# Moving fill-in work to earlier steps of an attention loop, and alternating its PSUM bank

## The reference

```python
def reference(x, w_qkv, w_out, w_up, w_down):      # x: (8, 4096, 1024), float32
    x = layernorm(x + attention(x, w_qkv, w_out))  # 16 heads of 64, causal softmax
    h = gelu(ternary_linear(x, w_up))              # rms-normalised input, weights -1/0/1
    x = layernorm(x + ternary_linear(h, w_down))   # d_ff = 4096
    return x
```

## Time and profile before

| | us |
|---|---|
| median of 3 runs | 3507.16 |
| lowest, highest | 3487.97, 3547.02 |
| profiled execution | 3440.04 |
| its span, slowest core | 3438.5 |

### The profile page before, as it was taken

One profiled execution on the slowest core, in us unless ns is written; L12 is line 12 of the kernel. 1 busy time (PEld: TensorE's weight loads), 2 busy tenths in 40 slices (PEclk: granted clock), 3 DMA queues, 4 the chain that ended last, 5 costly groups with the idle time before them and its releaser, 6 DMA issues. The chain is left out here.

```text
span 3438.5 us, 52708 instructions; the slowest of 8 cores (3428.3 to 3438.5 us)
## 1 busy us (share of the span) xinstructions
PE 2666.4 (78%) x19808; PEld 1328.1 (39%) x19808; DVE 970.6 (28%) x2483; ACT 1857.3 (54%) x2165; POOL 116.0 (3%) x231
## 2 busy tenths in 40 slices
PE   5995456677777777777777788334599999999998
PEld 2443123233333344344334444222344444444444
DVE  5443343333332322321211110454411111111111
ACT  2453113346576777777887888355443434443443
POOL 0000000000000000000000000000000000000000
PEclk9998667677777877878887755656699999999999
DMA  6666101010100101001000000343311111111111
GB/s 135 156 159 140 31 7 50 13 50 13 38 26 20 44 1 38 26 1 38 26 1 13 26 13 1 116 156 106 90 41 37 47 47 44 34 47 47 46 31 37
DMA packets 54922, 171.26 MB, mean 50 GB/s; under 512 B 6545, under 2 KB 6546, under 8 KB 54674
## 3 DMA queue, kind: packets, MB, share of 16 engines
q1 hardware_dynamic: 37730, 134.33, 12.2%
q0 software_dynamic: 16944, 33.56, 6.3%
HBM read 167.87 MB, written 33.55 MB: 59 GB/s over the span
## 5 line engine op out<-in xcount | busy, mean ns | idle before, releaser
L38 ACT ACTIVATE p_sb<-sc,negC 128x1024 bf16<-128x1024 f32 (+3 forms) x1152 | 1162.2, 1041 | 506.1 <-PE pvB L38 489.4
L38 PE MATMUL sc<-QT,KT 64*128 64x512 bf16 (+3 forms) x2304 | 530.8, 453 | 193.2 <-ACT p_sb L38 189.3
L38 PE MATMUL dwn<-wdnT,hTs 128*128 128x512 bf16 x2048 | 459.1, 380 | 8.8 <-ACT hTs L38 8.8
L38 PE MATMUL upq<-wupT,x1Ts 128*128 128x512 bf16 x2048 | 454.0, 380 | 6.5 <-DVE x1Ts L38 2.0
L38 PE MATMUL pvA<-VS,p_sb 128*128 128x65 bf16 x4224 | 372.9, 215 | 57.0 <-DVE recs L38 24.6
L38 PE MATMUL pvB<-VS,p_sb 128*128 128x65 bf16 x4224 | 375.5, 216 | 39.1 <-DVE attO L38 39.1
L38 PEld LDWEIGHTS pvA<-VS,p_sb 128*128 128x128 bf16 x4224 | 220.5, 107 | 396.6 <-issue 393.2
L38 ACT ACTIVATE h_sb<-upq,r_all 128x512 bf16<-128x512 f32 x256 | 175.2, 685 | 227.5 <-PE upq L38 224.6
L38 PEld LDWEIGHTS upq<-wupT,x1Ts 128*128 128x128 bf16 x2048 | 198.5, 98 | 256.5 <-issue 23.3
L38 PEld LDWEIGHTS dwn<-wdnT,hTs 128*128 128x128 bf16 x2048 | 195.8, 98 | 233.8 <-issue 15.7
L38 PEld LDWEIGHTS sc<-QT,KT 64*128 64x128 bf16 x2304 | 132.8, 96 | 374.6 <-issue 346.0
(11 more groups left out here) (107 smaller groups left out, 1874.2 us busy)
## 6 DMA issues: line engine op xcount, KB each, us to landing
wr<-w_up SPq DMA_DIRECT2D x64, 512.0 KB, 4.8
wr<-w_down SPq DMA_DIRECT2D x64, 512.0 KB, 4.1
xb<-x POOLq DMA_DIRECT2D x64, 256.0 KB, 3.9
xfy<-x SPq DMA_DIRECT2D x32, 512.0 KB, 3.4
x1spill<-xfy SPq DMA_DIRECT2D x32, 512.0 KB, 2.6
x1f<-x1spill SPq DMA_DIRECT2D x32, 512.0 KB, 5.4
out<-outs SPq DMA_DIRECT2D x32, 512.0 KB, 6.2
x1b<-x1spill POOLq DMA_DIRECT2D x32, 256.0 KB, 3.6
```

The lines of the kernel that those rows point to most:

```text
L38: getattr(self.real, op)(*args, **kw))
```

## The change

The bank of the transposes alternates: tiles with even number in the chunk go to bank 0, odd ones to bank 1, in `emit_qtrans`, `emit_proj_trans` and the preamble of chunk 0. Items are drained from k = 2 on instead of k = 5, and where nj > 16 at even steps instead of odd ones; budgets are as before. And before an `emit_proj_mm` of tile ti, `force_ln` emits the waiting layernorm items up to tile ti - 2, so that the load of xfy for which it waits has been issued.

```diff
@@ emit_qtrans, and alike in emit_proj_trans and the preamble of chunk 0
+                    mk = "mm6" if tt % 2 == 0 else "mm7"
+                    mo = 1024 * (tt % 2)
-                    t.wait(st2["mm6"])
+                    t.wait(st2[mk])
-                        t.transpose(mmp_b[:, 128 * ch:128 * ch + 128],
+                        t.transpose(mmp_b[:, mo + 128 * ch:
+                                          mo + 128 * ch + 128],
-                                  mmp_b[:, 0:1024].rearrange(
+                                  mmp_b[:, mo:mo + 1024].rearrange(
-                    st2["mm6"] = ("qxTe", ti)
+                    st2[mk] = ("qxTe", ti)
@@
+                def force_ln(ti):
+                    def tkey(q):
+                        return 4 * q[0][1] + q[0][2] if q else 10 ** 9
+                    while min(tkey(pend_ln), tkey(pend_ln2)) <= ti - 2:
+                        q = pend_ln2 if tkey(pend_ln2) <= tkey(pend_ln) \
+                            else pend_ln
+                        f2, c2, t2 = q.pop(0)
+                        f2(c2, t2)
@@ drain_in, and alike in drain_end
+                        if fn is emit_proj_mm:
+                            force_ln(4 * cc + tt)
@@
-                            elif p >= 1 and k >= 5 and (k % 2 == 1
+                            elif p >= 1 and k >= 2 and (k % 2 == 0
                                                         or nj <= 16):
                                 drain_end(p - 1,
                                           budget=(2 if nj <= 12 else 1))
```

More of the change, by code:

```diff
@@ L522, in emit_proj_trans @@
                     v.tensor_copy(aTs[:, ti % 2],
-                                  mmp_b[:, 0:1024].rearrange(
+                                  mmp_b[:, mo:mo + 1024].rearrange(
                                       "p (c n) -> p c n", n=128))
                     v.mark(("aTe", ti))
-                    st2["mm6"] = ("aTe", ti)
+                    st2[mk] = ("aTe", ti)
                 def emit_proj_mm_a(cc, tt):
@@ L636, in phase2 @@
                                    x_hbm[128 * ti:128 * ti + 128, :])
+                            mk = "mm6" if tt % 2 == 0 else "mm7"
+                            mo = 1024 * (tt % 2)
                             t.wait(("xb2", ti))
                             t.wait(("c", 6))
-                            t.wait(st2["mm6"])
+                            t.wait(st2[mk])
                             for ch in range(8):
                                 t.transpose(
-                                    mmp_b[:, 128 * ch:128 * ch + 128],
+                                    mmp_b[:, mo + 128 * ch:
+                                          mo + 128 * ch + 128],
                                     xb2[:, ti % 2, 128 * ch:128 * ch + 128],
```

## The result

The changed kernel takes **0.9855 of the time before, with a 95% interval from 0.9832 to 0.9877**: 1.45% faster, some 50 us. The medians are 3470.8 us against 3487.79; they also hold executions in which one half of the chip ran at a lower clock, which the ratio leaves out (those of the changed kernel that it keeps took 3388.68 to 3396.28 us). The profiled execution took 3392.37 us, against 3440.04. The forecast was -38.5 us, 1.1%, from the same sum. What it called the limit of a measurement, 2%, was too coarse: the interval above is 0.45% wide.

A forecast was written before the change was run, and what follows sets the result against it. ScalarE's exps set the pace, with 506 us idle before them. The terms summed to -38.5 us: 3401.5 from the profiled 3440.04, or 3468 on the median's scale, 1.95% higher; range 3405 to 3530 us.

The forecast's parts named there:

- the limit of a measurement, 2%: Whole kernel: a measurement can tell about 2% from no change, 70 us.
- Chunk 0: Items moved from the chunk's end into pairs 1 to 7: 35.4 us saved, pairs lengthened, -11.7 us net.
- Chunks 1 and 2: Earlier items cost less in the pairs and chunk 1's bare end shrinks: -11.2 and -7.1 us.
- The chain through y: Pair 2: next chunk's first transposes wait for the projection's scale, spill and reload, holding up scores; +18 us.
- Rival (c): Pair 2: the wait for y costs double, also holding masks and the next copy; 3487 us, chance 0.14.
- the clock: Pair starts: TensorE's higher clock may return one item earlier; -7 us, an eighth of 56.
- the next M now takes the 1.0 to 1.7: Chunks 3 to 6: step 2's matmul item is nearly hidden, the next costs 1.0 to 1.7; regular pairs win 0.3 us.
- a bound of 56: Most the clock could bring if it never fell at pair starts: 2 us in each of about 28 pairs.
- without a gap from T - 1 to about T + 7.5: Pair start: TensorE works unbroken at 1.2 GHz over this stretch; T is the end of the previous pair's last products.
- Rival (a): Pair starts: the clock stays up because the moved matmuls fill TensorE's idle 2 us; -88 us, 3418 us, chance 0.17.
- Rival (b): Regular pairs of chunks 1 to 6: the clock no longer comes back; 3526 us, up to 3555, chance 0.14.
- The bank: Preamble, chunk 1's pair 0 and the end: alternating banks spare second transposes' 0.94 us wait for the copy; -2.9 us.

The follow-up runs named there:

- e1: Kernel before with only the alternating bank and `force_ln` added, items drained at the old steps; 0.9975 of the kernel before.
- e7: Changed kernel, next chunk's four `emit_qtrans` items ahead of the last projection tile from chunk 1's pairs on; no ratio, fastest execution 3361.77 us against 3388.68.
- E5: Changed kernel with items of nj > 16 drained at even steps from 4 instead of from 2; 0.9952 of the kernel before.
- e6: Changed kernel with items of nj > 16 drained at odd steps from 3; 1.0011 of the kernel before.
- e10: Kernel before plus four unread matmuls at step 2 in pairs 4 to 7 of chunks 4 to 6, no item moved; 0.9969 of the kernel before.
- e4: Changed kernel plus four unread matmuls at each of steps 2 and 4 in pairs 3 to 7 of chunk 7; 0.9806 of the kernel before.
- e2: Changed kernel with early draining only where nj > 16 (chunks 4 to 7), short chunks from step 5; 0.9933 of the kernel before.

## Why the prediction came out as it did

**Chunk 0: right in kind, too large.** -11.7 forecast for the moved items, -9.5 measured; e1 gives 3.0 of it to the bank, so the items alone won 6.5. Pairs take 9.9 us (10.4 forecast), some 16 us without exps remain at the end (12 to 15). The pair with the Xs was mis-sized: 14.7 instead of 10.3 us. I had counted the third and fourth load, 4 us from their buffers, but not that the first two are issued by POOL behind its masks of pair 0, at 412.17, and land at 416.9.

**Chunks 1 and 2: the sum right by luck**, -17.1 measured for -16.3 with the chain. The bare 8.4 us between chunks 1 and 2 are gone (1.6), and C costs 2.3 inside (2.8 forecast; 8.4 less 2.8 is 5.6, not the 5.2 of the sum). Pairs 4 to 7 of chunk 1 fell from 19.5, 16.3, 19.4, 24.3 to 13.3, 11.9, 11.3, 14.5: more than the 3.1-for-5.2 of the forecast, since V N cost 1.0 there and the M M of pairs 6 and 7 run at 1.00. These four pairs won 28.5 us, where the block's -8.4 and C's -5.2 had been counted. That paid for pairs 2 and 3, 35.5 and 26.8 us instead of 26.3 and 18.4, 17.7 more, where some +4 had been counted: into them items moved, and the first X costs 9.1 us of idle time (median over the cores); before the change it cost 6.7, so the chain's share is an estimated +2.4, where I had put +1.0. Two errors of about 14 us cancelled.

**The chain through y: right in place.** Forecast 5 to 7 us of idle time before the exp of step 6; it is 8.1 to 8.4, more than that. Forecast +4 a pair; pair 2 grew by 2.2, 5.7, 1.3 and 3.2 in chunks 3 to 6, with an N gone from it in chunk 5, 12.4 in all for a forecast of 15.8. Rival (c), twice that, did not happen. I had argued the chain can't be shortened; e7 shows that it need not be, only not waited for.

**The term that failed: the clock, and with it the regular pairs.** The step of the prediction that failed was "the next M now takes the 1.0 to 1.7, because ScalarE has no lead then. So a regular pair wins only 0.3", and "I take an eighth, -7" of a bound of 56. Pairs 1, 5, 6 and 7 of chunks 4 to 6 fell by 19.1 us, 1.6 each, where 0.3 and a share of the 7 were counted, some 0.55: 12.5 us of the 15.8 by which these chunks missed. Here the start of chunk 4, pair 5 after the change:

```profile
1168.03 1.90 PE L38 MATMUL mmp<-xTs,wq 128*128 128x512 bf16 x4
...
1171.16 2.12 ACT L38 ACTIVATE p_sb<-sc,negC 128x1024 bf16<-128x1024 f32 x2 [1.32 <-PE pvB L38]
...
1171.64 1.03 PE L38 MATMUL mmp<-xTs,wq 128*128 128x512 bf16 x4
...
1173.44 3.21 ACT L38 ACTIVATE p_sb<-sc,negC 128x1024 bf16<-128x1024 f32 x3 [0.16 <-PE pvB L38]
```

M at step 2 takes 1.90 at 1.2 GHz and costs nothing (1.32 of idle time; 1.48 without it). The M at step 4 takes 1.03 at 2.4 GHz and costs 0.16, in place of 1.0 to 1.7. I had both facts, that M takes 0.95 less at the higher clock and that TensorE would be "without a gap from T - 1 to about T + 7.5", and still priced the second M as if the clock were low. The place where the clock comes back decided whether that M was dear, and it was a chance to be weighed, not an eighth to be taken. E5, e6 and e10 show it from three sides.

**The place on the scale.** The sum, 3401.5 us, was moved up by 1.95% to the median of three executions, and its range, 3405 to 3530, stands on that scale. The profiled execution of the changed kernel took 3392.37, 9 us below the sum and below the range; taken as a ratio to 3507.16, the result is 3456 and within it.

**Rival (a)** was half right: its mechanism, a filled gap, is what happened; but the clock does fall at the pair's start, from before T, and comes back sooner, so that it brought some 12 us in nine pairs (e10), not 56 in 28. **Rival (b)** occurred in single pairs only: in chunk 3, pair 4 went from 20.5 to 24.4 us and from 0.78 to 0.64, because TensorE now waits for an N's square (4.09 us of idle time on core 2), and the clock is low from there to the end of the pair. With the 2.2 of pair 2 this is why chunk 3 won nothing. The Trainium skill (TensorE: Matmul & The Clock Gate, A second HAM failure mode: psum-queue depth-cycling) says of a kernel that cycles through PSUM banks that frequent short pauses between its groups of matmuls make the clock swing between its two levels. The traces agree: filling one pause of about 2 us took chunk 4, pair 6 from 0.83 to 0.95 in e10, with nothing else moved.

**The bank: right in kind, short in size**, -8.6 for -2.9: the transposes at the bare end of chunk 0 (3.1 us) were not counted.

What stays open: why four matmuls at step 4 of a chunk 7 pair bring the clock back on two cores and not on six; why pair 4 of e4 stayed at 0.58 with what raised pairs 3 and 5; and how the gain of pairs 3 and 4 of chunks 4 to 6 divides between the clock and the moved N and V. The 2.4 us of chunk 7 (3.8 in e2) are in pairs 1 and 2, where the last projection tiles now stand at step 2: 39.2 and 38.3 us became 36.4 and 37.1.

## What to carry to other kernels

In these runs TensorE's wait for the epilogue was a free place for filled-in work, and worth more than free: work there decided how soon the higher clock came back for what followed, even work whose result nobody reads. Look for such a wait and try it, place by place, since in e10 the same work behind a V cost 3.2 us in one pair. Move items by two questions, then: does this one fill a pause that recurs every turn, and does it stand in an in-order queue in front of a chain (spill, reload, sum) that was only just started? If it does the latter, put other items between, as e7 did.

## What was not expected of the hardware

- Pairs 4 to 7 of chunk 7 ran at 1.2 GHz throughout (0.50), with TensorE busy for 35.0 of pair 5's 40.6 us. Four matmuls more, 1.9 us of work at step 2, made that pair 34.9 us at 0.94.
- The same four matmuls gave 34.9 us in pair 5 at step 2 (40.7 without them), 42.0 in pair 6 at step 4 (40.7), and 36.5 in pair 7 at step 5 (39.9). Before this, I would have counted work added to a stream that looks 86% busy as a cost.
